# Attention values in four column groups of the matmul array, and gate blocks moved into the maxima's phase

## The reference

```
x = x + tanh(g) * attention0(context, values = norm(x))
x = x + tanh(g) * experts0(norm(x))        # 8 experts, dense: sigmoid(gate) * up, then down, weights of the best two
# attention 1: 16 heads
scores = q_r . k_r ;  attn = softmax(scores)         # 256 queries x 256 keys per head
ctx_c = attn @ kv_rope                               # 64 numbers per head and query
out = (ctx_c . w_kc_kv) @ Wo.T                       # folded before into one matrix Go
x = x + tanh(g) * out
x = x + tanh(g) * experts1(norm(x))        # 8 experts, only the best two per row: batches 0 to 2 sorted by expert
```

## Time and profile before

| | |
|---|---|
| median of 3 runs | 462.15 us (461.87 to 463.34) |
| profiled execution | 462.53 us, span 460.7 us |
| PE busy | 391.8 us (85%) |
| DVE busy | 261.1 us (57%) |
| ACT busy | 248.2 us (54%) |
| POOL busy | 135.8 us (29%) |

### The profile page before, as it was taken

How to read it: one execution, slowest core, us unless ns; L and a number is a source line. 1 busy time by engine, 2 the same in 40 slices (tenths; PEclk the granted TensorE clock), 3 DMA queues, 4 the chain that set the end, 5 groups by cost and what they waited for, 6 DMA issues and landing times. The chain is left out here.

```text
span 460.7 us, 7898 instructions
## 1 busy us (share of the span) xinstructions
PE 391.8 (85%) x2691; PEld 330.3 (72%) x2691; DVE 261.1 (57%) x732; ACT 248.2 (54%) x507; POOL 135.8 (29%) x140
## 2 busy tenths in 40 slices
PE   1659993957989888988998898967999699999996
PEld 0325691546689777988777896766899589898885
DVE  0889434346723366823539623648874258555795
ACT  1013787418289649389466698534456245554332
POOL 4724200006201137102047011153448850000650
PEclk9999997869599999999999999989999989999999
DMA  5996800292011002011011020003236432311321
GB/s 153 303 331 198 104 2 0 56 329 48 1 25 25 3 0 48 1 25 25 1 25 25 1 48 1 2 23 91 71 97 203 153 110 92 95 68 60 91 93 46
DMA packets 30743, 35.37 MB, mean 77 GB/s; under 512 B 5712, under 2 KB 25792, under 8 KB 30448
## 3 DMA queue, kind: packets, MB, share of 16 engines
q1 hardware_dynamic: 26304, 28.11, 20.2%
q0 software_dynamic: 4400, 6.75, 6.6%
HBM read 25.61 MB, written 7.60 MB: 72 GB/s over the span
## 5 line engine op out<-in xcount | busy, mean ns | idle before, releaser
L1416 PE MATMUL bank<-kv,probs 128*128 128x128 f32 x512 | 67.6, 275 | 5.4 <-ACT negmT L1009 4.9
L1416 PEld LDWEIGHTS bank<-kv,probs 128*128 128x128 f32 x512 | 62.5, 192 | 6.2 <-issue 6.2
L1036 ACT ACTIVATE probs<-bank 128x512 f32<-128x512 f32 x64 | 37.5, 593 | 17.2 <-PE bank L1396 17.2
L1868 DVE TENSOR_REDUCE negm<-bank 128x2 f32<-128x512 f32 x64 | 41.4, 689 | 5.1 <-PE bank L1375 4.6
L1395 PE MATMUL bank<-Qs,Kh 128*128 128x256 f32 x128 | 39.0, 326 | 0.0
L1375 PE MATMUL bank<-Kh,Qs 128*128 128x256 f32 x128 | 32.2, 346 | 7.6 <-ACT fold_d L1019 3.0
L940 ACT ACTIVATE gu_all<-bank 128x512 bf16<-128x512 f32 x44 | 25.9, 593 | 19.7 <-PE bank L1199 19.6
L751 POOL TENSOR_TENSOR W<-w_in,W 128x512 fp32r<-128x512 f32 x24 | 30.0, 1280 | 21.3 <-issue 21.2
L740 POOL TENSOR_SCALAR veps<-mv 128x2 f32<-128x2 f32 x12 | 2.7, 226 | 111.9 <-DVE mv L1612 111.9
L1396 PE MATMUL bank<-Qm,Kl 65*128 65x256 f32 x128 | 33.5, 284 | 0.0
L1356 PE MATMUL bank<-f2s,Mq 128*128 128x256 f32 x192 | 29.2, 308 | 4.9 <-DVE f2s L1852 2.5
(11 more groups left out here) (213 smaller groups left out, 915.0 us busy)
## 6 DMA issues: line engine op xcount, KB each, us to landing
Qm<-Qs SPq DMA_DIRECT2D x32, 128.0 KB
xs<-f3A SPq DMA_DIRECT2D x1, 2432.0 KB, 9.9
Qm<-xs SPq DMA_DIRECT2D x19, 128.0 KB, 2.1
ys<-y SPq DMA_DIRECT2D x19, 128.0 KB, 2.0
w_q<-in_wq SPq DMA_DIRECT2D x2, 1024.0 KB, 18.1
w_o<-in_woT SPq DMA_DIRECT2D x1, 2048.0 KB, 10.9
w_in<-in_L_ffn_Wg SPq DMA_DIRECT2D x8, 256.0 KB, 4.0
w_in<-in_L_ffn_Wu SPq DMA_DIRECT2D x8, 256.0 KB, 2.9
```

The costliest lines, as they stand in the source:

```text
L1036: done(act.activation(flat(pT[:, n % 3]), bank1(b, FILL_ST + h)[:], ACT.Exp), "p_ready")
L1416: ins = pe.matmul(bank_v(b, h // 2)[:, at:at + P], pT[:, n % 3, lt, t * P:(t + 1) * P], kv_all[:, frm:frm + P], start=(lt == 0), stop=(lt ...
L1868: done(dve.tensor_reduce(negm[:, :, max_at(h)], rows(bank1(b, FILL_S + h)), AX.X, ALU.max, negate=True), "m_ready")
```

## The change

Four edits belong together, two ride along.

1. Values are computed for four heads (a quad) at once. The weights are now 32 columns (ones for the denominators, then the first and the last 32 columns of the keys' values), the moving data are the probabilities of one head, 256 columns, and head k of the quad writes partitions 32k to 32k + 31. The result comes out already turned, so `turn_ctx` and the whole copy go. Three steps per quad lie at set heads (DEN_AT, PV_AT). `probs` has eight buffers in place of three, and an exponential waits for the quad two before.
2. VectorE inverts 128 x 256 denominators, replicated over 32 partitions by the ones (REC_AT), and scales 128 x 512 into SBUF (MUL_AT). ScalarE copies the rounded part from there.
3. Seven of the next batch's eleven gate blocks lie in the maxima's phase, four beside the first twelve heads.
4. To make room, `w_in` has five windows, and SP's loads are ordered to suit: loads 0 to 4 first, 5 to 7 and 8 to 10 ahead of the last batch's late queries, 11 and up behind them.
5. `of_r` issues the first halves of two heads, then their second halves; `g_fold` writes quads.
6. Tiles have four y buffers and a third hTs of their own.

```diff
-        spread(a, NP + 1, f, 3)
-        spread(a, 12, f, J0 + 1 - 3)
+        spread(a, NP + 1, f, 7)
+        spread(a, 12, f, J0 + 1 - 7)
...
+DEN_AT = (5, 9, 13, 18)
+PV_AT = ((6, 10, 14, 16), (7, 11, 15, 17))
+REC_AT = (6, 10, 14, 18)
+MUL_AT = (8, 12, 16, 18)
+CTX_AT = (9, 13, 17, 19)
...
-        NWIN = 7
+        NWIN = 5
...
-            for k in range(7, 10):
+            for k in range(5, 8):
                 load_w1(k)
             for n in range(2):
                 maxima_in(B - 1, n)
-            for k in range(10, 13):
+            for k in range(8, 11):
                 load_w1(k)
             for n in range(2, 4):
                 queries_in(B - 1, n)
                 maxima_in(B - 1, n)
-            for k in range(13, 22):
+            for k in range(11, 22):
                 load_w1(k)
...
-                        if n >= 3:
-                            act.wait_ge(S_["pv_ready"], n - 2)
+                        if n >= 8:
+                            act.wait_ge(S_["den_ready"], (n - 8) // 4 + 1)
+                            act.wait_ge(S_["pv_ready"], (n - 8) // 4 + 1)
...
-                        done(act.activation(flat(ctxs[:, 0, 2 * k:2 * k + 2]), bank_c(b)[:], ACT.Copy), "cT_hi")
-                        if b < B - 1:
-                            done(act.activation(wait_full(act, b, 4 + k), bank_c(b)[:], ACT.Copy), "cT_full")
+                        done(act.activation(flat(ctxs[:, 0, 2 * k:2 * k + 2]), full[k % 2], ACT.Copy), "cT_hi")
...
-                    for h in range(4 * q, 4 * q + 4):
-                        pe.matmul(o, w_qra[:, h], w_kqa[:, h], start=True, stop=False)
-                        ins = pe.matmul(o, w_qrb[half(h), h // 2], w_kqb[half(h), h // 2], start=False, stop=True)
+                    for pr in range(2 * q, 2 * q + 2):
+                        for h in (2 * pr, 2 * pr + 1):
+                            pe.matmul(o(h), w_qra[:, h], w_kqa[:, h], start=True, stop=False)
+                        for h in (2 * pr, 2 * pr + 1):
+                            ins = pe.matmul(o(h), w_qrb[half(h), pr], w_kqb[half(h), pr], start=False, stop=True)
...
+                def in_quad(q, o, weights, sig):
+                    for lt in range(T):
+                        for k in range(4):
+                            ins = pe.matmul(o[QD * k:QD * k + QD], weights(lt), pT[(NH * b + 4 * q + k) % 8][:, lt],
                                             start=(lt == 0), stop=(lt == 1))
...
+                    in_quad(q, bank_den(b)[:, 0:S], lambda lt: ones[:], "den_ready")
...
+                    in_quad(q, bank_v(b, q)[:, part * S:(part + 1) * S],
+                            lambda lt: kv[:, b * T + lt, part * QD:(part + 1) * QD], "pv_ready" if part else None)
...
-                        done(dve.reciprocal(rden[:, m % 2], o[:, :, :, DC]), "pv_step")
+                        done(dve.reciprocal(rec[:, m % 2], bank_den(b)[:, 0:S]), "rec_ready")
...
+                        done(dve.tensor_tensor(wait_full(dve, b, 4 + q).rearrange("p (a s) -> p a s", a=2),
+                                               bank_v(b, q)[:].rearrange("p (a s) -> p a s", a=2),
+                                               rec[:, m % 2, None, :].to_broadcast([P, 2, S]), ALU.mult), "ctx_ready")
```

More of the change, by code:

```diff
@@ L301, in passing @@
             return layer1.enter_context(nc.sbuf_tensor(name, shape, dt))
-        ctxn = passing("ctxn", [P, T, NH, DC])
+        probs_b = passing("probs_b", [P, 5 * T * S])
+        rec = passing("rec", [P, 2, S])
+        pT = [w[:, n * T * S:(n + 1) * T * S].rearrange("p (t s) -> p t s", t=T) for w, m in ((probs, 3), (probs_b, 5)) for n in range(m)]
         ctxs = passing("ctxs", [P, 2, NP, S], F32R)
@@ L392, in flamingo @@
         scattered = sem("scattered")
-        y_out = [sem(f"y_out_{n}") for n in range(2)]
+        y_out = [sem(f"y_out_{n}") for n in range(4)]
         stored = sem("stored")
@@ L482, in wait_full, with bank_v, bank_den @@
                 pb, k = divmod(n, SPLITS)
-                if k < 4:
+                if k < 4 and pb < B - 1:
                     eng.wait_ge(S_["q_split"], 8 * pb + 2 * (k + 1))
+                elif k < 4:
+                    eng.wait_ge(S_["cT_lo"], NQ * pb)
                 else:
-                    eng.wait_ge(S_["cT_lo"], 4 * pb + k - 3)
+                    eng.wait_ge(S_["cT_lo"], NQ * pb + k - 3)
             return full[(SPLITS * b + i) % 2]
[L489 to L495, removed]
+        def bank_v(b, q):
+            return bank[(7, 4 if b < B - 1 else 3)[q % 2]]
+        def bank_den(b):
+            return bank[0 if b < B - 1 else 4]
         def qm_at(h):
@@ L763, in gather @@
             def gather():
-                for par in range(2):
-                    pool.wait_ge(y_out[par], 16 * ((SORTED + 1 - par) // 2))
+                for n in range(4):
+                    pool.wait_ge(y_out[n], 16 * ((SORTED + 3 - n) // 4))
                 for b in range(NS):
@@ L1442, in attn1 @@
                         turn_max(1)
-                    if 2 <= h <= NH + 1:
-                        values(h - 2)
-                    if h >= 7 and (h - 7) % 4 == 0:
-                        turn_ctx((h - 7) // 4)
+                    if h in DEN_AT:
+                        denominators(DEN_AT.index(h))
+                    for part in range(2):
+                        if h in PV_AT[part]:
+                            values(PV_AT[part].index(h), part)
                     if h < NH + 3:
@@ L1901, in attn1 @@
+                    for k in range(NQ):
+                        if h == min(CTX_AT[k] + 1, NH + 3):
+                            split_ctx(k)
                     if h < NH + 3:
```

146 lines of the change are left out of this document (64 added, 82 removed).

## The result

The changed kernel takes 477.35 us (median of 4, 474.28 to 484.64) beside 462.52 for the kernel before on the same chip: a ratio of 1.0288, 95% interval 1.0248 to 1.0328. The forecast was 456 us, range 446 to 468. It was wrong in sign and outside its range.

The account below looks back on a forecast made before the run. ScalarE was taken to set the pace in the first twelve heads, TensorE close behind. From 462.53 us: -2.5 (fold) - 3 x (5.2 + 0.5 - 2.2) + 6.5 = -6.5, so 456 us, range 446 to 468.

Parts of the forecast that it names:

- Part 2: Reordered fold of a, two heads side by side: 2.5 us saved once, bounds 0 and 5.8.
- Part 1: Values and denominators in four column groups on TensorE: 1.05 us a group, 3.1 us less per batch, giving only room.
- Part 3: VectorE's 128x256 reciprocals: 2.0 us each, delaying each passage to the next batch by 2.2 us.
- Part 4: Gate blocks moved: twelve-head stage 23.0 to 15.9 us, maxima's phase 1.9 longer, net 5.2 us saved per batch for three batches.
- Part 5: Five weight windows for seven, last batch: late loads delay weight copies and outputs, +6.5 us, bounds +3 and +12.
- Rival D: Column groups on TensorE run only two at a time: 489 us; chance 0.05.
- Rival A: VectorE's 128x256 reciprocal costs only 0.42 us: 448 us; chance 0.23.
- the 13.9 of the sum: TensorE's predicted work in the twelve-head stage, 13.9 us, below ScalarE's 15.9, so ScalarE still binds.
- the 1.33 wait: TensorE's 1.33 us wait ahead of the first values for the copied maxima, forecast to move off.
- rival B: Gates only change place: maxima's phase grows by 6 us for 1.9, total 468, deciding from 4.1; chance 0.10.
- the named copy: ScalarE's weight copy of expert 3 in the last batch, forecast at 345.6 in place of 340.5.
- Rival C: Last batch loses +14 for +6.5: TensorE idles, lower clock, copies wait for their loads; 463.5 us; chance 0.12.

## Why the prediction was wrong, by its steps

The error of 19.1 us in the span (from -6.5 to +12.6) divides so, up to rounding:

| step | forecast | measured | error |
|---|---|---|---|
| to the queries of batch 1 (part 2, and one batch of parts 1, 3, 4) | -7.5 | -6.4 | 1.1 |
| values and gates with short reciprocals (parts 1, 4), batches 1 and 2 | -11.4 | -7.0 | 4.4 |
| reciprocal's length (part 3), batches 1 and 2 | +5.9 | +13.1 | 7.2 |
| last batch (part 5) | +6.5 | +13.0 | 6.5 |

The measured -7.0 is 126.0 us with short reciprocals against 133.0; +13.1 is 139.1 against 126.0. Each is the difference of single traces.

**Part 1** was right: 1.07 us a group at the full clock, all four side by side. Rival D falls. The drain at a change of tiling mode of which the Trainium skill speaks ("TensorEngine Tiling (Array Packing)", Key Properties) is inside that number.

**Part 2** is not borne out: -1.5 us to the queries of batch 0 in this trace, but +2.3 in another with the same setup, and no gain by its own run.

**Part 3** is the step that failed most: "I take +2.2 per passage to the next batch, both effects together". The duration was right, 1.75 us for 2.0. The estimate of 2.3 us that the prediction drew from the Trainium skill ("VectorE: DVE Perf Modes", First, the fixed hardware budget) lies further off. The reach was not right: batches 1 and 2 are 13.1 us longer for 5.9, and the fourth reciprocal alone costs 4.8 us in each. I followed the reciprocal to ScalarE's query copies and stopped at "the router and the maxima's start all stand behind it". Behind it the delay grows: router operations slide under GpSimd's query splits, the first maxima are late, TensorE idles, and its clock falls. Rival A priced a short reciprocal at 448; the runs with short ones have a median of 460.2 and begin at 451.6, so parts 4 and 5 were off as well. Part 3 alone doesn't turn the sign: without its 7.2 us of error the change is still 5 us slower.

**Part 4**, with part 1, gave 7.0 us in batches 1 and 2 where 11.4 were forecast, and its parts were off by more. Of the 13 instructions and 7.1 us counted, ten and 4.6 us left ScalarE's stage (42 to 32, 21.3 to 16.7 us busy), but the stage went from 23.0 to 21.2 us, not 15.9. TensorE is busy 17.8 us there for the 13.9 of the sum. By an estimate from the mean clock, the lower level takes up to 0.16 x 21.2 = 3.4 us of that; the sum also has a head's scores at 0.5 where the earlier trace rows give 0.56. And seven gates leave ScalarE behind at the first exponentials: "the 1.33 wait moves off", but the 2.32 us wait takes its place, and it is there with short reciprocals too (2.33). How much of the missing 5.3 us each costs is not shown. The maxima's phase grew by 4.0 us, at the 4.1 from which rival B decides, yet B's cause is refuted: gates alone cost it 1.0 us, and the fourth reciprocal the other 2.9 (14.4 us with that one short).

**Part 5**: the chain was right to the rows it named: five windows alone cost 5.9 us for the 6.5 forecast, with a wait of 5.31 us at the named copy, and once that wait was lifted, the next was at expert 5's, as written. What failed is that it stood for the whole last batch. Of its 13.0 us the windows alone make 5.2 (60.3 us to the outputs for 55.1), and reciprocals some 4 (64.2 us with short ones, a subtraction of 2.99 us within it, 68.1 with long). What makes the 3.9 us between 60.3 and 64.2 no run separates. Rival C gave +14 for +13.0 measured, and its marks are there (idle times of 4.36 and 4.05 us, outputs at a clock of 0.68). But C took all else as forecast, so its total was 463.5.

The 8 us subtraction was in no part. The earlier trace rows hold its condition, GpSimd's three splits in a row; I did not ask which VectorE operations lose their PSUM operand by the change. It makes some executions 8 us longer and costs the others nothing.

Left open: how the lower clock and the idle stretches divide the 2.9 us of the maxima's phase beyond that bound of 1.7, what the last batch's other 3.9 us are, and why batch 2 is 2 to 3 us longer than batch 1 in the kernel before and in the changed one.

## What to carry to other kernels

A longer operation on an engine with room on average is priced where its queue is a chain: follow it to the next engine's first late instruction, and to what the delayed small operations then fall beside. When a change moves an operand from PSUM to SBUF, look up what GpSimd does at that time. And a change bought with buffers should be priced twice, alone and with the delays that the rest of the change adds to the same stage.

## Of the hardware, not expected

- A 128x512 subtraction on VectorE with both inputs in SBUF took 8.06, 7.99 and 7.50 us when six GpSimd TENSOR_TENSORs (7.36 us) ran beside it, 4.41 and 2.99 us beside a row of three, and 0.63 to 0.69 us with one input in PSUM or GpSimd idle. In all five it ends 0.55 to 0.56 us behind GpSimd's last one, wherever it started: it is held until they end, not slowed in proportion. In the trace of 484.64 us it was held though it starts 0.15 us ahead of them.
- Two 128x8 operations on VectorE: 1.47 us beside a GpSimd split, 0.36 without.
- A reciprocal of 128x256 from PSUM takes 1.753 us and of 128x64 0.55: by an estimate from the two, 6.3 ns an element and 0.15 us.
- On ScalarE the Ln of 128x256 takes 0.38 us and the Exp 0.42, together under half of VectorE's reciprocal; where they wait for each other and for TensorE, as at the end of batch 2, nothing is left of the difference.
